# Filter spectra of a convolution block from high and low float32r parts instead of four-byte floats

## The chip, the core and the metric

The kernel runs on one core of a Trainium2 chip. A core has TensorE (PE; its weight loads are listed as PEld), VectorE (DVE), ScalarE (ACT), GpSimd (POOL) and SyncE (SP), each with a queue of its own that runs in order, and 16 DMA engines. The metric is the device time of one launch in microseconds (us). The profile shows one execution; its span is counted from the first to the last instruction.

## The reference

An image batch `x` of 16 x 128 channels x 16 x 16 runs through a convolution with filters that depend on the image, an attention and a mixture of experts. Only the first part is touched. Cut to what matters:

```
query   = x.reshape(b, c, hw)                      # x group-normalised
key     = softmax(einsum('bchw,oc->bohw', x, K_w) + K_b)
filters = einsum('bcn,bnk->bck', query, key)       # 7 x 7 taps per image and channel
filters = einsum('bcij,oc->boij', filters, conv0_w) + conv0_b
filters = relu(layernorm(filters) * ln_w + ln_b)
filters = einsum('bcij,oc->boij', filters, conv1_w) + conv1_b
out     = depthwise_conv(x, filters, padding=3)    # 7 x 7, per image and channel
t = x + out;  t = t + attention(ln(t));  t = t + moe(ln(t))   # top 2 of 8 experts
```

## The kernel before

The images are taken in 8 pairs. The depthwise convolution is done in the frequency domain on a 19 x 19 grid: TensorE multiplies the image (`features_spectrum`, L1095) and the filters (`filter_spectrum`, L1163) by constant matrices of cosines and sines, VectorE multiplies the two spectra (`products`, `spectrum`, `rest_products`), and `image` (L1178) transforms back. The 181 frequencies need four result tiles: real and imaginary parts of 121 frequencies (tiles 0 and 1) and two tiles with the other 60 (124 rows each). Tiles 0 and 1 of the filter lie in PSUM bank `bank_d0`, tiles 2 and 3 in `bank_d1`. The constant matrix for the filter is `tapf`, 49 taps by 121 + 121 + 124 + 124 = 490 columns; the filter `filt` has 49 taps by 2 images by 128 channels.

Every engine has its own program, written by hand; the order in it is the order in which it runs, and semaphores tie the engines together. A loop over nine rounds `i` is a pipeline: in round `i` pair `i` is at stage n (normalisation), `i-1` at a (keys and filter taps), `i-2` at b (filter), `i-3` at c (convolution), `i-4` at d (attention), `i-5` at e (routing) and `i-6` at f (dispatch). After the loop the rest of the pairs stands in a list written out for each engine, and then come 71 blocks of 128 tokens through the experts.

What surrounds the change:

- VectorE's `filter_of(b)` (L820) adds the bias to the filter from PSUM and writes `filt`, near the end of round `i`. Behind it on VectorE come `slot_indices_of` (L789), `z_of(c)` (L838), `attention_sum(d)` (L852), `attention_stats(d)` (L662 to L669) and `weight_differences` (L678, L679). The statistics let GpSimd compute `ln2_rstd` (L459; the profile calls it `ln_rstd`).
- In the next round VectorE's `rows_of(e)` (L723) waits for that, writes the normalised rows, and TensorE's `router_input(e)` (L1103) transposes these rows. Then follow `scores` (L1170), `router` (L1110), and on VectorE `logits_of` (L730).
- TensorE in a round: transposes of `gbuf` (L1204), keys (L1209), `first_conv` (L1145), `filter_spectrum` (L1163) of the filter made in the round before, transposes of `z` (L1140), `filter_mean` (L1149), `features_spectrum` (L1095), `router_input` (L1103), `scores` (L1170), `router` (L1110), `filter_square` (L1153), an expert's weights (L1188), `kprob` transposes (L1277), group mean (L1283), `image` (L1178), ranks (L1120, L1122), L1296, L1303, `attention` (L1132), and `filter_of` (L1158), which makes the filter that L820 reads.
- `keep_busy` (L1090) are products whose results nobody reads.
Of the kernel before, what the change touches and what calls it, by code (L numbers as in the profile page):

```python
# [29 lines left out]
F32R = mybir.dt.float32r  # L30
# [6 lines left out]
P = 128  # L37
# [3 lines left out]
KKP = 64  # L41
# [33 lines left out]
def constants():  # L75
# [27 lines left out]
    tapf[:KK] = np.concatenate([re[:, :WIDE], im[:, :WIDE], both(re, im), both(im, re)], 1)  # L103

# [22 lines left out]
def build(nc, a_in, out):  # L127
# [9 lines left out]
    with ctx:  # L137
# [12 lines left out]
        tapf = cst("tapf")  # L150

# [11 lines left out]
        c1_b = sb("c1_b", [KK, C])  # L163
# [48 lines left out]
        frelu = sb("frelu", [P, 2, KK])  # L212
        filt = sb("filt", [KK, 2, C])
# [75 lines left out]
        filt_psum, filt_done = sem("filt_psum"), sem("filt_done")  # L289
        ghat_psum, ghat_done = sem("ghat_psum"), sem("ghat_done")  # L290
# [64 lines left out]
        with nc.Block() as block:  # L355
# [148 lines left out]
            def _(act):  # L504
                act.dma_start(b1c[:, :], a_in["b1c"]).then_inc(ld_bias, 16)
                act.dma_start(bgv[:, :], a_in["bgv"]).then_inc(ld_bias, 16)
                act.dma_start(c1_b[:, :], a_in["c1_b"].partition_broadcast(KK)).then_inc(ld_c1b, 16)
# [21 lines left out]
                def first_conv(b):  # L529
# [6 lines left out]
                    last.then_inc(f0_done, 1)  # L536

# [30 lines left out]
                for i in range(rounds):  # L568
# [52 lines left out]
                    if n is not None:  # L621
# [7 lines left out]
                        last.then_inc(g_done, 1)  # L629
                first_conv(7)  # L630
# [6 lines left out]
                weights_exp(4)  # L637
                rest_spectrum(7)
# [16 lines left out]
            def _(dve):  # L655
                dve.memset(ones[:, :], 1.0)
                dve.memset(either[:, TILES, :], 0.0)

# [152 lines left out]
                def rectified(b):  # L811
                    dve.wait_ge(fln_done, b + 1)
                    dve.tensor_scalar(frelu[:, :, :], fln[:, :, :], 0.0, None, ALU.max).then_inc(frelu_done, 1)

                def filter_of(b):
                    if b == 0:
                        dve.wait_ge(ld_c1b, 16)
                    dve.wait_ge(filt_psum, b + 1)
                    after(dve, what_psum, 2 * b)
                    dve.tensor_tensor(filt[:, :, :], bank_b[0:KK, 256:512].rearrange("k (s c) -> k s c", s=2),  # L820
                                      spread(c1_b[:, :], 1, 2), ALU.add).then_inc(filt_done, 1)

# [50 lines left out]
                for i in range(rounds):  # L873
# [111 lines left out]
                    if c is not None:  # L985
                        z_of(c)
                    if d is not None:
# [42 lines left out]
                second_choice(4)  # L1030
# [52 lines left out]
            def _(pe):  # L1083
# [770 lines left out]
```

## Time and profile before

| | us |
|---|---|
| runs | 331.98, 333.33, 332.0 (median 332.0) |
| profiled execution, its own time | 332.57 |
| its span | 330.6 |
| TensorE busy / weight loads | 296.0 / 236.5 |
| VectorE busy | 232.8 |
| ScalarE busy | 144.5 |
| GpSimd busy | 164.7 |

Busy time is the sum over the whole span, and matmuls are pipelined, so that a busy TensorE says little about whether it sets the time. From 7 us on TensorE runs almost without a gap; the rounds 3 to 8 start on it at 36.3, 53.5, 72.3, 92.9, 113.5 and 134.0 us, the list after the loop at 154.4, and the first expert block at 200.9.

### The profile page before, as it was taken

What the parts mean: (1) busy time and instruction counts of PE and PEld (TensorE: products, weight loads), DVE (VectorE), ACT (ScalarE), POOL (GpSimd) and SP (SyncE); (2) the same over time, 40 slices, a digit from 0 to 9 for tenths busy, and PEclk for the clock granted to TensorE, in tenths of its full rate; (3) what the DMA queues carried; (4) which work ended last, traced back from release to release, by engine and by line L of the source; (5) the groups of instructions that cost most, each with busy time, mean ns of one, the idle gap of its engine ahead of it and who ended that gap; (6) DMA issues with size and microseconds to landing.
All of it is one profiled execution on the core that took longest, in us unless ns stands there. A gap on an engine that the chain in (4) does not pass through costs nothing.

```text
span 330.6 us, 7141 instructions
## 1 busy us (share of the span) xinstructions
PE 296.0 (90%) x1733; PEld 236.5 (72%) x1733; DVE 232.8 (70%) x1012; ACT 144.5 (44%) x465; POOL 164.7 (50%) x187
## 2 busy tenths in 40 slices
PE   0889999999999999999998986999999999999910
PEld 0557777688777778778876764876888888888810
DVE  2424375679788797877889795688666676767883
ACT  1344343625237352461420424555566666666600
POOL 3000002021163746636748765667777777676650
PEclk9979999999999999999999998799999999999985
DMA  6751423050211811001101113334433333335937
GB/s 189 281 171 45 133 76 102 4 168 5 80 48 34 285 39 35 16 24 36 34 25 50 44 41 93 99 98 108 113 92 104 89 105 108 97 84 153 353 131 250
DMA packets 29920, 33.39 MB, mean 101 GB/s; under 512 B 5064, under 2 KB 23836, under 8 KB 29626
## 3 DMA queue, kind: packets, MB, share of 16 engines
q1 hardware_dynamic: 24608, 23.64, 24.3%
q0 software_dynamic: 4352, 8.60, 7.6%
q10 hardware_dynamic: 922, 0.71, 0.7%
q8 instruction: 16, 0.26, 0.4%
q14 instruction: 22, 0.18, 0.2%
HBM read 21.69 MB, written 11.68 MB: 101 GB/s over the span
## 4 chain that ended last, share of the span: by engine, by line
PE 65%; DVE 16%; issue 6%; POOL 4%; DMA 3%; ACT 3%; DVEq 1%; POOLq 0%; SPq 0%; ACTq 0%
PE bank L1784 7%; PE bank L1178 6%; PE bank L1095 6%; PE bank L1188 4%; PE bank L1759 4%; PE bank L1764 4%; PE bank L1760 4%; PE bank L1773 4%; PE bank L1163 3%; PE bank L1170 3%; PE bank L1090 3%; POOL rows_dram L429 3%; PE bank L1754 2%; DVE ys L1699 2%; PE bank L1132 2%
## 5 line engine op out<-in xcount | busy, mean ns | idle before, releaser
L1492 POOL DMA_INDIRECT moe_dram<-ys,xs x71 | 70.0, 987 | 29.0 <-issue 19.5
L429 POOL DMA_INDIRECT rows_dram<-row,slot x56 | 55.6, 993 | 24.6 <-issue 13.5
L1784 PE MATMUL bank<-w_all,gatedt 128*128 x284 | 44.1, 278 | 0.1
L1580 ACT ACTIVATE silu<-bank 128x256 f32<-128x256 f32 x71 | 27.2, 383 | 33.3 <-PE bank L1764 32.9
L1699 DVE SCALAR_TENSOR_TENSOR ys<-b_all,xs,bank 128x128 f32<-128x128 f32 x71 | 24.7, 348 | 23.0 <-issue 20.5
L1716 DVE SCALAR_TENSOR_TENSOR gated<-bank,xs,silu 128x256 f32<-128x256 f32 x71 | 34.2, 482 | 7.4 <-ACT silu L1580 3.4
L1784 PEld LDWEIGHTS bank<-w_all,gatedt 128*128 128x128 f32 x284 | 37.7, 193 | 0.3 <-issue 0.3
L1759 PE MATMUL bank<-w_high,x_high 128*128 x71 | 34.8, 491 | 2.6 <-ACT x_high L1567 2.6
L440 POOL TENSOR_TENSOR frstd<-fvar,minus_half 128x2 f32<-128x2 f32 x7 | 4.9, 706 | 52.4 <-DVE fvar L802 52.4
L1764 PE MATMUL bank<-w_high,x_low 128*128 x71 | 29.5, 415 | 0.4
L1178 PE MATMUL bank<-zhat,const 121*128 121x256 f32 (+1 forms) x128 | 29.6, 383 | 0.1
L1760 PE MATMUL bank<-w_low,x_high 128*128 x71 | 28.4, 400 | 0.0
L1773 PE MATMUL bank<-const,gated 128*128 128x128 f32 x142 | 27.9, 278 | 0.6 <-DVE gated L1716 0.6
L1571 ACT ACTIVATE gatedt<-bank 128x256 f32<-128x256 f32 x71 | 26.9, 379 | 1.2 <-PE bank L1773 1.1
L1773 PEld LDWEIGHTS bank<-const,gated 128*128 128x128 f32 x142 | 19.6, 142 | 9.5 <-DVE gated L1716 2.2
L1178 PEld LDWEIGHTS bank<-zhat,const 121*128 121x128 f32 (+1 forms) x128 | 23.6, 189 | 3.7 <-issue 0.5
L1567 ACT ACTIVATE x_high<-bank 128x128 fp32r<-128x128 f32 x71 | 19.7, 277 | 10.5 <-PE bank L1754 3.6
L1090 PE MATMUL bank<-const 128*128 128x256 f32 x82 | 23.5, 416 | 0.0
L1095 PE MATMUL bank<-gt,const 128*121 128x256 f32 (+1 forms) x96 | 22.8, 385 | 0.0
L1690 DVE TENSOR_TENSOR x_low<-bank,x_high 128x128 fp32r<-128x128 f32 x71 | 20.3, 286 | 3.3 <-ACT x_high L1567 3.2
L446 POOL TENSOR_TENSOR gn_rstd<-gn_var,minus_half 128x2 f32<-128x2 f32 x8 | 5.7, 715 | 32.1 <-DVE gn_var L966 32.1
L1764 PEld LDWEIGHTS bank<-w_high,x_low 128*128 128x128 f32 x71 | 13.6, 191 | 8.5 <-DVE x_low L1690 2.9
(203 smaller groups left out, 623.2 us busy)
## 6 DMA issues: line engine op xcount, KB each, us to landing
xs<-rows_dram SPq DMA_DIRECT2D x71, 66.0 KB, 1.9
xc<-in_x SPq DMA_DIRECT2D x8, 256.0 KB, 3.1
wgv<-in_wg SPq DMA_DIRECT2D x8, 256.0 KB, 2.8
wgv<-in_wv SPq DMA_DIRECT2D x8, 256.0 KB, 3.1
xt<-in_xt SPq DMA_DIRECT2D x4, 512.0 KB, 4.9
xt<-moe_dram SPq DMA_DIRECT2D x8, 256.0 KB, 4.5
moe_dram<-ys,xs POOLq DMA_INDIRECT x71, 2.3
const<-in_const SPq DMA_DIRECT2D x1, 1123.0 KB, 9.6
```

Of the source, the lines that this page charges most:

```text
L429: pool.indirect_dma_start(rows_dram, bass.IndirectOffsetOnAxis(ap=slot[:, f % 2, 2 * t + k:2 * t + k + 1], axis=0), row[:, f % 2, t, k, :] ...
L1090: pe.matmul(bank, ident, const[:, 0:2 * P], start=True, stop=True)
L1095: last = pe.matmul(bank_s[r // 2][0:tile_rows[r], r % 2 * 2 * C:(r % 2 + 1) * 2 * C], fwd[:, h, tile_cols[r]], gt[:, b % 2, h, :], start=( ...
L1178: last = pe.matmul(bank_o[:, h * 2 * C:(h + 1) * 2 * C], inv[0:tile_rows[r], r, h * P:(h + 1) * P], zhat[0:tile_rows[r], r, :], start=(r = ...
L1492: pool.indirect_dma_start(moe_dram, bass.IndirectOffsetOnAxis(ap=xs[:, u, C + 1:C + 2].bitcast(U32), axis=0), ys[:, u, :], None, bounds_ch ...
L1699: dve.scalar_tensor_tensor(ys[:, u, :], b2_all[:, bass.ds(e * C, C)], xs[:, u, C:C + 1], bank_y[j % 2][:, 0:C], ALU.mult, ALU.add).then_in ...
L1716: dve.scalar_tensor_tensor(gated[:, j % 2, :], bank_h[j % 2][:, HID:2 * HID], xs[:, j % U, C:C + 1], silu[:, j % 2, :], ALU.mult, ALU.mult ...
L1759: pe.matmul(bank_h[j % 2][:, :], x_high[:, j % 2, :], w_high[:, bass.ds(e * (2 * HID), 2 * HID)], start=True, stop=False)
L1760: pe.matmul(bank_h[j % 2][:, :], x_high[:, j % 2, :], w_low[:, bass.ds(e * (2 * HID), 2 * HID)], start=False, stop=False)
L1764: pe.matmul(bank_h[j % 2][:, :], x_low[:, j % 2, :], w_high[:, bass.ds(e * (2 * HID), 2 * HID)], start=False, stop=True).then_inc(S["h_psu ...
L1773: last = pe.transpose(bank_g[:, h * P:(h + 1) * P], gated[:, j % 2, h * P:(h + 1) * P], ident)
L1784: last = pe.matmul(bank_y[j % 2][:, 0:C], gatedt[:, j % 2, h * P:(h + 1) * P], w2_all[:, bass.ds(e * (2 * C) + h * C, C)], start=(h == 0), ...
```

## The change

The filter is written twice, to partitions 0 to 48 and 64 to 112 (`frelu` holds each tap twice, so that L1158 gives 113 rows, 15 of them zero taps with the bias). ScalarE copies all of it to a float32r tile, `filt_parts`, the high part (`filter_high`). VectorE then replaces partitions 64 to 112 by the difference between filter and high part (`filter_low`). The constant matrix is split once, at the end of round 2, into `tap_high` (which holds the taps twice as well) and `tap_low`. Each product of the spectrum becomes two in float32r: `tap_high` over 113 partitions, which sums high and low part of the filter, and `tap_low` with the high part over 49. The product of both low parts is left out. On TensorE the transposes of `z` move ahead of the spectra. After the loop `second_choice(4)` is written out, with `filter_low(7)` between its steps.

The constants and tiles:

```diff
+    tapf[KKP:KKP + KK] = tapf[:KK]
...
+        tap_high = sb("tap_high", [P, WIDTHS["tapf"]], F32R)
+        tap_low = sb("tap_low", [P, WIDTHS["tapf"]], F32R)
-        c1_b = sb("c1_b", [KK, C])
+        c1_b = sb("c1_b", [KKP + KK, C])
...
-        frelu = sb("frelu", [P, 2, KK])
-        filt = sb("filt", [KK, 2, C])
+        frelu = sb("frelu", [P, 2, 2, KKP])
+        filt = sb("filt", [KKP + KK, 2, C])
+        filt_parts = sb("filt_parts", [KKP + KK, 2, C], F32R)
```

ScalarE, with the calls at the end of a round (behind `gbuf`) and, last, after the loop (behind `weights_exp(4)`):

```diff
+                def filter_high(c):
+                    act.wait_ge(filt_done, c + 1)
+                    after(act, filt_low_done, low_of(c - 1))
+                    after(act, what_psum, 2 * c)
+                    act.activation(filt_parts[:, :, :].rearrange("k s c -> k (s c)"),
+                                   filt[:, :, :].rearrange("k s c -> k (s c)"), ACT.Copy).then_inc(filt_high_done, 1)
...
+                    if i == 2:
+                        act.wait_ge(ld_c2, 16)
+                        act.activation(tap_high[:, :], tapf, ACT.Copy).then_inc(filt_high_done, 1)
+                    if b is not None:
+                        filter_high(b)
...
+                filter_high(7)
```

VectorE, with the calls in a round (between `z_of(c)` and `attention_sum(d)`) and, last, after the loop:

```diff
+                dve.memset(frelu[:, :, :, :], 0.0).then_inc(filt_low_done, 1)
...
-                    dve.tensor_scalar(frelu[:, :, :], fln[:, :, :], 0.0, None, ALU.max).then_inc(frelu_done, 1)
+                    dve.tensor_scalar(frelu[:, :, :, 0:KK], spread(fln[:, :, :], 2, 2), 0.0, None, ALU.max).then_inc(frelu_done, 1)
...
+                def filter_low(c):
+                    dve.wait_ge(filt_high_done, high_of(c))
+                    dve.tensor_tensor(filt_parts[KKP:KKP + KK, :, :], filt[KKP:KKP + KK, :, :], filt_parts[KKP:KKP + KK, :, :],
+                                      ALU.subtract).then_inc(filt_low_done, 1)
...
+                    if i == 2:
+                        dve.wait_ge(filt_high_done, 1)
+                        dve.tensor_tensor(tap_low[:, :], tapf, tap_high[:, :], ALU.subtract).then_inc(filt_low_done, 1)
+                    if b is not None:
+                        filter_low(b)
...
                 filter_of(7)
-                second_choice(4)
+                chosen_of(4)
+                either_of(4)
+                filter_low(7)
+                exp_sum_of(4)
+                exp_reciprocal_of(4)
+                weights_of(4)
```

TensorE; in the round `features_of_z(d)` with its waits now stands ahead of the last lines:

```diff
-                        last = pe.matmul(bank_b[0:KK, 256 + s * C:256 + (s + 1) * C], frelu[:, s, :], c1_t, start=True, stop=True)
+                        last = pe.matmul(bank_b[0:KKP + KK, 256 + s * C:256 + (s + 1) * C],
+                                         frelu[:, s, :, :].rearrange("p d k -> p (d k)")[:, 0:KKP + KK], c1_t, start=True, stop=True)
...
-                        last = pe.matmul(bank_d[half][0:tile_rows[r], r % 2 * 2 * C:(r % 2 + 1) * 2 * C],
-                                         tapf[0:KK, tile_cols[r]], filt[:, :, :].rearrange("k s c -> k (s c)"),
-                                         start=True, stop=True)
+                        into = bank_d[half][0:tile_rows[r], r % 2 * 2 * C:(r % 2 + 1) * 2 * C]
+                        pe.matmul(into, tap_high[0:KKP + KK, tile_cols[r]], filt_parts[:, :, :].rearrange("k s c -> k (s c)"),
+                                  start=True, stop=False)
+                        last = pe.matmul(into, tap_low[0:KK, tile_cols[r]], filt_parts[0:KK, :, :].rearrange("k s c -> k (s c)"),
+                                         start=False, stop=True)
...
-                        pe.wait_ge(filt_done, c + 1)
-                        if c == 0:
-                            pe.wait_ge(ld_c2, 16)
+                        pe.wait_ge(filt_low_done, low_of(c))
```

On TensorE, the start of a round from 5 on (the names are tiles; L1140 and L1184 are the transposes of `z`, L1163 and L1209/L1211 the spectra), before:

```order
L1145 MATMUL bank<-fraw,small 128x98 [waits fraw_done,pos_done,filt_done]
L1163 MATMUL bank<-filt,const 121x256 [waits zhat_done,wlow_done,prod_done,filt_done]
L1163 MATMUL bank<-filt,const 121x256
L1163 MATMUL bank<-filt,const 124x256 x2
L1140 MATMUL bank<-const,z 128x128 [waits qt_done,z_done,z2t_done,gt_done]
L1140 MATMUL bank<-const,z 128x128 x3
L1149 MATMUL bank<-fsum,const 128x2 [waits f0_done]
```

and now:

```order
L1189 MATMUL bank<-fraw,small 128x98 [waits fraw_done,pos_done,filt_done]
L1184 MATMUL bank<-const,z 128x128 [waits qt_done,z_done,z2t_done,gt_done]
L1184 MATMUL bank<-const,z 128x128 x3
L1209 MATMUL bank<-filt_parts,tap_high 121x256 [waits zhat_done,wlow_done,prod_done,filt_low_done]
L1211 MATMUL bank<-filt_parts,tap_low 121x256
L1209 MATMUL bank<-filt_parts,tap_high 121x256
L1211 MATMUL bank<-filt_parts,tap_low 121x256
L1209 MATMUL bank<-filt_parts,tap_high 124x256
L1211 MATMUL bank<-filt_parts,tap_low 124x256
L1209 MATMUL bank<-filt_parts,tap_high 124x256
L1211 MATMUL bank<-filt_parts,tap_low 124x256
L1193 MATMUL bank<-fsum,const 128x2 [waits f0_done]
```

Four products became eight, the transposes of `z` stand ahead of them, and the spectra wait for the low part in place of the filter itself.

On VectorE, the end of a round (`t` is the attention sum, `ln_raw` its statistics), before:

```order
L820 TENSOR_TENSOR filt<-bank,c_b 49x256 [waits what_psum,filt_psum]
L789 CAST slot<-slotf 128x8 [waits route_step]
L838 TENSOR_SCALAR z<-t,ln_mv,ln_rstd 128x128 [waits attn_psum,ln_rstd_done]
L838 TENSOR_SCALAR z<-t,ln_mv,ln_rstd 128x128 x3
L852 SCALAR_TENSOR_TENSOR t<-bank,arec,t 128x128 [waits attn_psum,arec_done]
```

and now:

```order
L849 TENSOR_TENSOR filt<-bank,c_b 113x256 [waits filt_low_done,filt_psum]
L815 CAST slot<-slotf 128x8 [waits route_step]
L872 TENSOR_SCALAR z<-t,ln_mv,ln_rstd 128x128 [waits attn_psum,ln_rstd_done]
L872 TENSOR_SCALAR z<-t,ln_mv,ln_rstd 128x128 x3
L854 TENSOR_TENSOR filt_parts<-filt,filt_parts 49x256 [waits filt_high_done]
L886 SCALAR_TENSOR_TENSOR t<-bank,arec,t 128x128 [waits attn_psum,arec_done]
```

One instruction stands between `z` and the attention sum, and it waits for ScalarE.

## Rows read from the trace of the kernel before

**Rows 1.** The page, section 4: shares of the chain that ended last.

```profile
PE 65%; DVE 16%; issue 6%; POOL 4%; DMA 3%; ACT 3%; DVEq 1%; POOLq 0%; SPq 0%; ACTq 0%
```

**Rows 2.** Stretches: busy us and count by engine, granted clock, DMA share, GB/s.

```profile
36.20:53.50 17.30, 17.24 (x87) 13.33 (x87) 9.88 (x40) 5.99 (x20) 2.40 (x3) 1.00 0.28 90
...
205.00:210.00 5.00, 4.74 (x20) 3.78 (x21) 2.98 (x13) 2.37 (x8) 3.78 (x5) 0.50 0.45 110
```

**Rows 3.** Chain of waits, round 7: start, length, piece.

```profile
115.10 1.92 PE bank L1163 x8
```

**Rows 4.** Timeline of TensorE, expert blocks: start, length, instruction, count.

```profile
240.29 0.39 PE L1760 MATMUL bank<-w_low,x_high 128*128 x1
240.52 0.39 PE L1764 MATMUL bank<-w_high,x_low 128*128 x1
...
240.97 0.61 PE L1784 MATMUL bank<-w_all,gatedt 128*128 x4
241.42 0.27 PE L1754 MATMUL bank<-const,xs 128*128 128x128 f32 x1
```

**Rows 5.** Timeline of all engines, round 7.

```profile
113.24 0.42 DVE L820 TENSOR_TENSOR filt<-bank,c_b 49x256 f32<-49x256 f32 x1 [0.82 <-PE bank L1158]
...
114.68 1.11 DVE L852 SCALAR_TENSOR_TENSOR t<-bank,arec,t 128x128 f32<-128x128 f32 x4
...
117.40 1.22 POOL L459 TENSOR_TENSOR ln_rstd<-ln_var,minus_half 128x4 f32<-128x4 f32 x1 [0.99 <-DVE ln_var L669]
...
118.65 1.27 DVE L723 TENSOR_SCALAR row<-t,ln_mv,ln_rstd 128x127 f32<-128x127 f32 x4 [0.30 <-POOL ln_rstd L459]
...
120.04 0.57 PEld L1103 LDWEIGHTS bank<-const,row 128*128 128x128 f32 x4
...
120.25 0.60 PE L1103 MATMUL bank<-const,row 128*128 128x128 f32 x4
...
120.67 0.41 DVE L701 TENSOR_TENSOR prod<-bank,ghat 121x256 f32<-121x256 f32 x1
...
120.89 1.99 PE L1170 MATMUL bank<-qt 128*128 128x256 f32 x8
...
121.00 0.41 DVE L702 TENSOR_TENSOR prod<-bank,ghat 121x256 f32<-121x256 f32 x1
...
122.83 0.74 DVE L870 BATCH_NORM_STATS2 gn_raw<-xc 128x6 f32<-128x256 f32 x2
...
123.71 0.19 DVE L730 COPY logits<-bank 128x32 f32<-128x32 f32 x1
```

**Rows 6.** Timeline of VectorE, rounds 5 and 8: reading the logits.

```profile
82.61 0.19 DVE L730 COPY logits<-bank 128x32 f32<-128x32 f32 x1 [0.28 <-PE bank L1110]
...
144.25 0.19 DVE L730 COPY logits<-bank 128x32 f32<-128x32 f32 x1 [0.80 <-PE bank L1110]
```

**Rows 7.** Groups by form: busy us, mean ns, idle time before.

```profile
L521 ACT ACTIVATE row<-row 128x512 f32<-128x512 f32 x8 | 5.0, 628 | 0.0
...
L813 DVE TENSOR_SCALAR frelu<-fln 128x98 f32<-128x98 f32 x8 | 1.7, 213 | 0.1
```

**Rows 8.** Timeline after the loop: VectorE, TensorE and GpSimd.

```profile
163.86 1.13 DVE L852 SCALAR_TENSOR_TENSOR t<-bank,arec,t 128x128 f32<-128x128 f32 x4 [0.58 <-PE bank L1132]
...
168.33 0.19 DVE L755 TENSOR_TENSOR either<-chosen 128x32 bf16<-128x32 f32 x1
...
169.56 1.12 PE L1163 MATMUL bank<-filt,const 49*121 49x256 f32 x4
...
170.62 0.19 PE L1120 MATMUL bank<-either,before 128*128 128x40 bf16 x1
...
170.94 0.16 DVE L773 TENSOR_TENSOR base<-base,bank 128x8 f32<-128x8 f32 x1 [0.88 <-PE bank L1122]
...
172.28 1.03 POOL L429 DMA_INDIRECT rows_dram<-row,slot  x1 [3.88 <-DVE slot L789]
...
205.26 0.79 PE L1759 MATMUL bank<-w_high,x_high 128*128 x1 [2.24 <-ACT x_high L1567]
```

More of the change, by code:

```diff
@@ L289, in build, with high_of, low_of @@
         filt_psum, filt_done = sem("filt_psum"), sem("filt_done")
+        filt_high_done, filt_low_done = sem("filt_high_done"), sem("filt_low_done")
+        def high_of(c):
+            return c + 2
+        def low_of(c):
+            return c + 3
         ghat_psum, ghat_done = sem("ghat_psum"), sem("ghat_done")
@@ L506, in _ @@
                 act.dma_start(bgv[:, :], a_in["bgv"]).then_inc(ld_bias, 16)
-                act.dma_start(c1_b[:, :], a_in["c1_b"].partition_broadcast(KK)).then_inc(ld_c1b, 16)
+                act.dma_start(c1_b[:, :], a_in["c1_b"].partition_broadcast(KKP + KK)).then_inc(ld_c1b, 16)
                 act.dma_start(router_b[:, :], a_in["router_b"].partition_broadcast(1)).then_inc(ld_router, 16)
@@ L818, in filter_of @@
                     dve.wait_ge(filt_psum, b + 1)
-                    after(dve, what_psum, 2 * b)
-                    dve.tensor_tensor(filt[:, :, :], bank_b[0:KK, 256:512].rearrange("k (s c) -> k s c", s=2),
+                    if b > 0:
+                        dve.wait_ge(filt_low_done, low_of(b - 1))
+                    dve.tensor_tensor(filt[:, :, :], bank_b[0:KKP + KK, 256:512].rearrange("k (s c) -> k s c", s=2),
                                       spread(c1_b[:, :], 1, 2), ALU.add).then_inc(filt_done, 1)
+                def filter_low(c):
+                    dve.wait_ge(filt_high_done, high_of(c))
+                    dve.tensor_tensor(filt_parts[KKP:KKP + KK, :, :], filt[KKP:KKP + KK, :, :], filt_parts[KKP:KKP + KK, :, :],
+                                      ALU.subtract).then_inc(filt_low_done, 1)
                 def image_sum(c):
@@ L1216, in _ @@
                         first_conv(b)
+                    if d is not None:
+                        after(pe, gt_done, through(i, A))
+                        after(pe, z2t_done, through(i - 1, E))
+                        after(pe, qt_done, d)
+                        features_of_z(d)
                     if c is not None:
-                        pe.wait_ge(filt_done, c + 1)
-                        if c == 0:
-                            pe.wait_ge(ld_c2, 16)
+                        pe.wait_ge(filt_low_done, low_of(c))
                         after(pe, prod_done, c)
@@ L1226, in _ @@
                         filter_spectrum(c, 1)
-                    if d is not None:
-                        after(pe, gt_done, through(i, A))
-                        after(pe, z2t_done, through(i - 1, E))
-                        after(pe, qt_done, d)
-                        features_of_z(d)
                     if b is not None:
@@ L1329, in _ @@
                 pe.wait_ge(wlow_done, EXPERTS)
+                pe.wait_ge(filt_low_done, low_of(6))
                 filter_spectrum(6, 0)
@@ L1347, in _ @@
                 features_spectrum(7, (2,))
-                pe.wait_ge(filt_done, 8)
+                pe.wait_ge(filt_low_done, low_of(7))
                 filter_spectrum(7, 0)
```

2 lines of the change are left out of this document (added).

## The prediction

> **What bounds the kernel now.** I read the chain of waits first: two thirds of it is TensorE [rows 1]. The stretches say where. The loop of nine rounds (here named by the program's `i`) fills TensorE: 17.24 us busy of 17.30 in round 3 [rows 2]. That busy time is no proof that each TensorE instruction counts, so I went on to the timeline of all engines in a full round (round 7; rounds 5, 6 and 8 repeat it), looking for waits that only just do not happen. From the round in which routing starts (5), there is a ring through VectorE: filter bias `filt` (L820, released by TensorE), `z`, attention sum L852, its statistics, the power on GpSimd L459, the rows L723, and then the transposes of these rows on TensorE, L1103. The rows end at 118.65 + 1.27 = 119.92, the weight load of L1103 starts at 120.04, its product at 120.25 [rows 5]. So the rows arrive 0.2 us before TensorE is free. Everything that TensorE does between the start of a round and L1103, the filter spectra L1163 among it, lies beside this ring, and may shrink by only 0.2 us before TensorE waits for the rows. In rounds 3 and 4 there is no routing and no L1103, and TensorE alone sets the time. After the loop a list in written order follows in which VectorE, GpSimd and TensorE hand on to each other; then 71 expert blocks, which the change leaves alone.
>
> **What each part costs.**
>
> *The spectra on TensorE.* Removed: per pair 4 products of four-byte floats, 8 hardware products, 1.92 us, so 0.24 each [rows 3] (eight such stretches, two of them split). Added: 8 products in float32r of 256 columns. The trace has float32r only with 512 columns: starts 0.23 apart (240.29, 240.52), which bounds it from above; the four four-byte products of 128 columns, each with its own weight load, start 0.45 / 4 = 0.113 apart [rows 4], which is the fastest pace of any pair of load and product in these rows. Half of the 512 columns gives 0.115, and that lies beside the lower row; I take 0.115, so 8 x 0.115 = 0.92 and 1.0 us less per pair. The upper end, 0.23, would be 1.84 and 0.08 less.
>
> *The high and low part.* ScalarE copies 113x256 (`filter_high`), VectorE subtracts 49x256 (`filter_low`). ScalarE's SBUF copy of 512 columns takes 628 ns [rows 7]; at 256 between 0.31 (half) and 0.63, I take 0.42. In round 7 `filt` ends at 113.66; the copy would end near 114.15, and VectorE comes to `filter_low` at 114.68, behind `z` [rows 5]. So the copy is hidden, with 0.5 us to spare; behind it on ScalarE queues only the copy of TensorE's transposes, which have to be made first anyway. `filter_low` is not hidden: it stands ahead of the attention sum, in the ring. Its like, L701 (two inputs, 256 columns), takes 0.41, but the next one, L702, starts 0.33 after it [rows 5]; I take 0.34. Queued behind it: attention sum, statistics, GpSimd's power, rows, L1103. Bounds: 0.33 and 0.41.
>
> *The doubled filter.* The weight load of L1158 grows from 49 to 113 columns; only the first of its loads is uncovered, and L1158 releases `filt`: between 0 and 0.11 (one load and product of rows 4), I take 0.05 per round. The bias on 113 partitions in place of 49 has the same columns: nothing. `frelu` doubles from 98 to 196 elements, 213 ns now [rows 7], so between 0 and 0.21 more, I take 0.1; in the loop VectorE idles afterwards for the image, which hides it.
> By the Trainium skill ("VectorE: DVE Perf Modes", "The perf-mode tier table (the rule you actually need)") a four-byte tensor_scalar within SBUF runs two elements a cycle; kept here, an estimate by that page is 0.05 for the 98 further elements, and 0.15 if reading the input twice loses the mode. No row decides it, and the sum changes by 0.05 either way.
>
> *Once.* `tap_high` and `tap_low` (490 columns) stand at the end of round 2, ahead of the first parts; the copy is like that of 512 columns, 0.63 [rows 7]. TensorE has its transposes, keys and first convolution to do meanwhile. I take a wait of 0.1 in round 3, between nothing and one such step, 0.6. The larger load of `c1_b` and the memset lie in the opening wait for data.
>
> *The move of the `z` transposes* ahead of the spectra costs nothing on TensorE: the same instructions, and VectorE had left `z` at 114.68 [rows 5], before the 115.10 at which the spectra, and now the transposes, follow on TensorE [rows 3].
>
> **The sum.** Rounds 3 and 4: -1.0 + 0.1 + 0.05 and -1.0 + 0.05, together -1.8. Rounds 5 to 8: the ring grows by 0.34 + 0.05 = 0.39 each, and gives back only what idles in it. Where do the rows go next? TensorE: L1103, then the scores L1170 at 120.89, where four products at 0.113 would have let it start at 120.70; with the 0.2 ahead of L1103, TensorE has room for 0.35. VectorE: from the rows' end it works without a pause to the image statistics, 122.83 + 0.74 = 123.57, and reads the logits (L730) at 123.71 [rows 5]: room for only 0.14. So VectorE becomes the later one in rounds 6 and 7. In round 5 its wait for the logits is 0.28, in round 8 (no image statistics) 0.80 [rows 6], there TensorE's 0.35 holds. Growth: 4 x 0.39 - (0.28 + 0.14 + 0.14 + 0.35) = +0.65. The loop as a whole: -1.15.
>
> After the loop: the attention sum L852 of pair 5 waits 0.58 for TensorE [rows 8]; VectorE itself comes later by 0.34 + 0.1 there, so it can move by -0.1, and the image of pair 6 with it. Then come the spectra of pair 7, L1163 at 169.56, four of them in 1.06 us up to the ranks at 170.62 [rows 8]; at 0.115 they take 0.5 less. `filter_low(7)` is ready before: it stands on VectorE behind `either`, which starts at 168.33 [rows 8]. The ranks release L773, which waits 0.88 for them, and that releases GpSimd's dispatch, which waits 3.88 for its slots [rows 8]; GpSimd then sets the pace to the next `z`. So -0.6 more. The spectra of pair 6 save nothing: the scores behind them wait for VectorE's centred filters, which come later by `filter_low`.
>
> Total -1.15 - 0.6 = -1.75 us. Against the profiled execution, 332.57 us (span 330.6 and 1.97 around it), that is 330.8. The median of the runs before is 332.0, 0.57 lower; from there **330.3 us**.
>
> **Rivals.**
> 1. *All of it is kept*: `filter_low` finds a pause and the rows come in time, so 1.0 goes in each of six rounds, and the list gives 0.6: 332.0 - 6.6 = 325.4. For it: TensorE's busy share. Against: 0.2 us ahead of L1103.
> 2. *The ring takes back more*: ScalarE's copy comes later than VectorE's `z`, or the waits on semaphores cost more, say 0.25 in each of rounds 5 to 8: 330.3 + 1.0 = 331.3. For it: a ring through three engines that has no slack. Against: 0.5 us of room for the copy.
> 3. *Slower: float32r of 256 columns keeps the pace of 512*, 0.23. Rounds 3 and 4 then give 0.16 less 0.2, nothing; rounds 5 to 8 cost 0.65, the list 0.15: +0.85, 332.9. The sum turns from gain to loss at about 0.19 per product. For it: no row shows 256. Against: 0.113 per load and product at half the columns with two passes.
> 4. *The clock.* In rounds 5 to 7 TensorE now idles some 1.2 us ahead of L1103. The granted clock is 1.00 in round 3 and 0.50, that is 1.2 GHz, from 205 to 210, behind the gap of 2.24 us that ends at 205.26 [rows 2, 8]; that stretch of 5 us did the work of 2.5. One such fall costs about 2.5: 332.8. Against it: the new gap is half as long.
> The Trainium skill ("TensorE: Matmul & The Clock Gate", "Part 1: The HAM clock gate (the "warmup" mystery)") says that "the default state is throttled, and activity releases the throttle", which speaks against a change that takes work from TensorE without shortening the round.
> 5. *It does not do what it says*: both products and all parts stand in the changed order, so no chance is given.
>
> **How the numbers follow.** Forecast 0.55 (own range 329.4 to 331.2), rival 1 0.06, rival 2 0.22, rival 3 0.09, rival 4 0.08. Half a per cent, 1.7 us, is about what a measurement of this kernel can tell from no change, so faster means below 330.3. The forecast lies on that edge: 0.32 of it faster, 0.23 same. Faster 0.32 + 0.06 + a little of rival 2 = 0.40. Rivals 3 and 4 lie within or just past +0.5%: half of 4 and a third of 3 and some unknown, slower 0.09. Same 0.51. The range leaves out rival 1 and the tail of 4: 328.7 to 332.8.
>
> **What would show it.** Right: 0.11 to 0.12 between the starts of the new products; a round 3 and 4 shorter by 0.9 each; rounds 6 and 7 not shorter, with TensorE idle about 1.2 us and released by the rows; no wait of VectorE for `filter_high` in the loop; the ranks of pair 4 about 1.8 us earlier. Wrong: rounds 6 and 7 shorter by 0.5 or more, starts 0.2 apart, a granted clock below 1.00 inside the loop, or the expert stage changed in length by more than a few tenths.

## The result

The changed kernel takes 343.6 us (median of four runs, 339.81 to 345.39) against 332.2 for the kernel before on the same chip, ratio 1.03 (95% interval 1.0255 to 1.0344). Ratios and intervals, here and below, leave out slow runs, those over 1.5% above the fastest of their kernel (here 345.39); medians and ranges do not. It is 11 us slower where 1.75 faster was forecast. The profiled execution after took 343.45 us (span 341.7; before 330.6).

The chain of waits after says again that TensorE sets the time, and more of it [rows 1]:

```profile
PE 68%; DVE 16%; DMA 5%; ACT 4%; issue 4%; DVEq 1%; POOL 1%; SPq 0%; POOLq 0%; ACTq 0%
```

So I cut both traces at the same places on TensorE: the start of each round, the first convolution of the list (L1145, now L1189) and the first `w_high` product of the expert blocks (L1759, now L1805). Columns as in [rows 2]; the number before the last two is the granted clock. After:

```profile
0.00:37.78 37.78, 25.91 (x115) 18.58 (x115) 12.98 (x61) 12.38 (x33) 5.59 (x24) 0.95 0.54 171
37.78:59.24 21.46, 20.68 (x86) 15.31 (x87) 11.49 (x44) 6.69 (x22) 2.40 (x3) 0.84 0.25 71
59.24:78.50 19.26, 18.53 (x100) 14.42 (x101) 11.61 (x47) 8.19 (x29) 2.40 (x3) 1.00 0.24 76
...
120.47:141.42 20.95, 20.20 (x117) 15.97 (x118) 17.78 (x95) 9.47 (x32) 11.72 (x12) 1.00 0.14 50
141.42:163.70 22.28, 21.44 (x113) 16.57 (x113) 16.68 (x86) 8.40 (x31) 11.02 (x11) 0.92 0.08 25
163.70:212.34 48.64, 45.40 (x253) 35.81 (x254) 41.89 (x227) 15.17 (x51) 31.67 (x32) 0.96 0.12 39
212.34:341.70 129.36, 112.11 (x715) 93.58 (x715) 90.71 (x284) 68.12 (x215) 84.50 (x87) 0.92 0.44 131
```

Before, the same stretches (round 3 starts at 36.26):

```profile
36.26:53.47 17.21, 17.21 (x87) 13.30 (x87) 9.85 (x40) 5.99 (x19) 2.40 (x3) 1.00 0.28 90
53.47:72.33 18.86, 18.25 (x102) 14.37 (x101) 10.91 (x46) 8.04 (x28) 2.40 (x3) 1.00 0.25 77
...
113.50:134.04 20.54, 19.93 (x117) 15.91 (x118) 17.19 (x93) 9.16 (x31) 11.72 (x12) 1.00 0.18 66
134.04:154.36 20.32, 19.48 (x114) 15.45 (x114) 16.14 (x85) 8.07 (x29) 11.01 (x11) 1.00 0.09 28
154.36:201.60 47.24, 43.53 (x253) 34.35 (x253) 40.73 (x224) 14.35 (x49) 31.64 (x32) 1.00 0.13 40
201.60:330.60 129.00, 111.09 (x715) 92.99 (x715) 90.42 (x284) 68.16 (x215) 84.55 (x87) 0.93 0.45 131
```

The difference of 11.1 us is made up of +1.5 in the opening, +4.25 in round 3, +0.4 in round 4, +1.2 in rounds 5 to 7 (0.4 each), +2.0 in round 8, +1.4 in the list, and +0.4 in the blocks. Two things stand out: a steady 0.4 per round at full clock, and stretches in which the clock is lower than before.

The steady part is in the spectra. TensorE in round 7 after (start, length, instruction), to be read beside [rows 3] and [rows 5]:

```profile
122.27 0.36 PE L1209 MATMUL bank<-filt_parts,tap_high 113*121 113x256 f32 x1
122.56 0.38 PE L1211 MATMUL bank<-filt_parts,tap_low 49*121 49x256 f32 x1
...
124.71 0.38 PE L1193 MATMUL bank<-fsum,const 128*128 128x2 f32 x2
...
127.62 0.60 PE L1147 MATMUL bank<-const,row 128*128 128x128 f32 x4
```

and its weight loads:

```profile
122.24 0.18 PEld L1209 LDWEIGHTS bank<-filt_parts,tap_high 113*121 113x121 f32 x1
122.56 0.18 PEld L1211 LDWEIGHTS bank<-filt_parts,tap_low 49*121 49x121 f32 x1
```

The products start 0.305 apart, not 0.115. Each weight load starts only where the product before gives way (at 122.56, 0.29 behind that product's start), so the load of 0.18 is laid in front of each product instead of beside the one before. Eight products take 2.44 in place of 1.92. L1147, the transposes of the rows, follows without a wait, and so it does in every round: the ring through VectorE never came to bound a round.

The other part begins in round 3. All engines after:

```profile
39.03 0.42 ACT L554 ACTIVATE filt_parts<-filt 113x256 fp32r<-113x256 f32 x1 [0.80 <-DVE tap_low L1023]
39.48 0.42 DVE L854 TENSOR_TENSOR filt_parts<-filt,filt_parts 49x256 fp32r<-49x256 f32 x1 [0.54 <-ACT filt_parts L554]
39.96 0.38 PE L1209 MATMUL bank<-filt_parts,tap_high 113*121 113x256 f32 x1 [0.54 <-DVE filt_parts L854]
...
41.34 0.57 PE L1209 MATMUL bank<-filt_parts,tap_high 113*124 113x256 f32 x1
```

The high part waits for the split of the taps, TensorE waits 0.54 for the low part, and from about the fourth product on everything takes longer. The clock there:

```profile
40.90:49.00 8.10, 8.10 (x23) 5.92 (x23) 3.02 (x10) 0.97 (x3) 0.00 (x0) 0.58 0.00 0
```

8.10 us at 0.58 do the work of 4.70, if the work goes with the clock; so, by this estimate, 3.4 of the 4.25 lost in round 3 are the clock.

### The profile page after: what moved, and what is told of

It reads as the page before. It is cut to its first block, busy times and chain, and to the rows that moved or that the text cites. A ratio compares the mean times of both kernels' runs of the same rounds, so it can differ in the third digit from the quotient of the medians.

```text
span 341.7 us, 7169 instructions
## 1 busy us (share of the span) xinstructions
PE 304.7 (89%) x1733; PEld 242.2 (71%) x1733; DVE 238.6 (70%) x1022; ACT 147.4 (43%) x474; POOL 164.7 (48%) x187
## 4 chain that ended last, share of the span: by engine, by line
PE 68%; DVE 16%; DMA 5%; ACT 4%; issue 4%; DVEq 1%; POOL 1%; SPq 0%; POOLq 0%; ACTq 0%
PE bank L1225 9%; PE bank L1830 7%; PE bank L1139 7%; PE bank L1235 4%; PE bank L1805 4%; PE bank L1810 4%; PE bank L1806 4%; PE bank L1819 4%; PE bank L1217 4%; PE bank L1211 3%; PE bank L1134 3%; PE bank L1209 2%; DMA small<-in_small 2%; PE bank L1800 2%; PE bank L1154 2%
## 5 line engine op out<-in xcount | busy, mean ns | idle before, releaser
L1805 PE MATMUL bank<-w_high,x_high 128*128 x71 | 35.4, 499 | 2.0 <-ACT x_high L1613 2.0
L1225 PE MATMUL bank<-zhat,const 121*128 121x256 f32 (+1 forms) x128 | 30.5, 392 | 0.0
L1225 PEld LDWEIGHTS bank<-zhat,const 121*128 121x128 f32 (+1 forms) x128 | 24.6, 197 | 3.6 <-DVE t L886 0.2
L1139 PE MATMUL bank<-gt,const 128*121 128x256 f32 (+1 forms) x96 | 26.4, 430 | 0.0
L1134 PE MATMUL bank<-const 128*128 128x256 f32 x82 | 24.3, 427 | 0.0
L1139 PEld LDWEIGHTS bank<-gt,const 128*121 128x121 f32 (+1 forms) x96 | 19.5, 210 | 3.6
```

Of the source, the lines that this page charges most:

```text
L1134: pe.matmul(bank, ident, const[:, 0:2 * P], start=True, stop=True)
L1139: last = pe.matmul(bank_s[r // 2][0:tile_rows[r], r % 2 * 2 * C:(r % 2 + 1) * 2 * C], fwd[:, h, tile_cols[r]], gt[:, b % 2, h, :], start=( ...
L1225: last = pe.matmul(bank_o[:, h * 2 * C:(h + 1) * 2 * C], inv[0:tile_rows[r], r, h * P:(h + 1) * P], zhat[0:tile_rows[r], r, :], start=(r = ...
L1805: pe.matmul(bank_h[j % 2][:, :], x_high[:, j % 2, :], w_high[:, bass.ds(e * (2 * HID), 2 * HID)], start=True, stop=False)
```

## The experiments

Theories A to D, as the expectation below numbers them, are ways in which the load could lose its place beside the product: narrow weights, unequal rows, float32r itself, or one pace per product.

**The pace by itself.** Behind the last block, which leaves everything ahead of it as it is:

```diff
+        def group(weights, moving, banks_, rows, n):
+            for _ in range(8):
+                pe.matmul(bank_h[0][:, 0:2 * P], ident, ident_mean, start=True, stop=True)
+            for k in range(16):
+                w, m = weights[k % 2], moving[k % 2]
+                pe.matmul(banks_[k // 2 % 2][0:rows, 0:n], w, m, start=(k % 2 == 0), stop=(k % 2 == 1))
...
+        group((tap_high[0:113, 0:121], tap_low[0:49, 0:121]), (parts, parts[0:49, :]), two, 121, 256)
+        group((tap_high[0:113, 0:121], tap_low[0:113, 0:121]), (parts, parts), two, 121, 256)
...
```

> The changed kernel with twelve groups of 16 products put behind its last block, each group behind 8 four-byte products of 128x128 by 256 columns that keep the clock; the rest is as it is. It measures the disputed pace, start to start, by itself: in the loop the float32r spectra stand 0.305 us apart, and the load of the next weights (0.18) begins only when the product before has ended. Groups in order: (1) as in the loop, 113 and 49 rows by turns, 121 weight columns, 256 columns; (2) 113 rows in both; (3) 49 rows in both; (4) 113 rows, 128 weight columns; (5) 128 rows, 128 weight columns, 256 columns; (6) the same, 512 columns; (7) the same, 128 columns; (8) 128 rows, 121 weight columns; (9) 128 rows, 64 weight columns; (10) four-byte, 49 rows, 121 weight columns, 256 columns; (11) four-byte, 113 rows; (12) four-byte, 128x128. Theory A (weights narrower than 128 columns are not loaded ahead): 0.30 in groups 1, 2, 3, 8, 9, and 0.11 to 0.13 in 4 and 5. Theory B (a change of the number of rows stops it): 0.30 in group 1 alone, 0.11 to 0.13 in 2 to 5 and 8. Theory C (a float32r load never runs beside the product before it, so that each product costs its load of 0.18 and its columns): 0.29 to 0.31 in groups 1 to 5 and 8, 0.23 to 0.25 in group 7, 0.38 to 0.41 in group 6. Theory D (the forecast's own upper rival, float32r keeps one pace per product whatever its columns): 0.23 in 2 to 7. All theories: four-byte groups 0.22 to 0.25.

TensorE behind the last block (L1857 are the 8 four-byte products between the groups, L1860 the groups; lines of a group of equal shape are one row of 16):

```profile
326.34 0.38 PE L1860 MATMUL bank<-filt_parts,tap_low 49*121 49x256 f32 x1
326.65 0.38 PE L1860 MATMUL bank<-filt_parts,tap_high 113*121 113x256 f32 x1
...
330.94 5.41 PE L1857 MATMUL bank<-const 128*128 128x256 f32 x16
...
336.43 0.28 PE L1860 MATMUL bank<-filt_parts,tap_high 113*121 113x256 f32 x1
336.55 0.28 PE L1860 MATMUL bank<-filt_parts,tap_low 113*121 113x256 f32 x1
...
338.10 3.62 PE L1857 MATMUL bank<-const 128*128 128x256 f32 x16
...
357.82 4.07 PE L1860 MATMUL bank<-w_high,x_high 128*128 128x512 f32 x16
...
391.86 7.07 PE L1860 MATMUL bank<-filt,const 113*121 113x256 f32 x32
```

113 and 49 rows by turns: 0.31 apart. 113 in both, or 49 in both: 0.12. Narrow weights at equal rows change nothing (121 and 64 columns: 2.25 and 2.24 for 16). Theory B alone stands; A, C and D fall. The row of 512 columns, 4.07 for 16 or 0.24 apart, shows that the forecast's halving was right for equal rows (128 columns are no faster than 256, though: 1.92 from the first start of 16 to the start behind them). The fillers, as I call the 8 four-byte products, tell something more: behind the group of unequal rows the same 8 four-byte products took 5.41 in place of 3.62, at a granted clock of 0.66, so partly at 1.2 GHz:

```profile
325.94:330.94 5.00, 5.00 (x18) 2.84 (x16) 2.76 (x5) 0.00 (x0) 0.30 (x1) 1.00 0.61 191
330.94:336.00 5.06, 5.06 (x17) 4.16 (x17) 2.90 (x6) 0.00 (x0) 0.00 (x0) 0.66 0.69 258
```

**Which rows.** The same with other pairs, `group((x_high[0:a, 0, 0:128], x_high[0:b, 1, 0:128]), (w_high[0:a, 0:256], w_high[0:b, 0:256]), ...)`, where `a` and `b` are the numbers of rows:

> As the run that measured the pace by itself, with other groups of 16 float32r products of 256 columns behind the last block, 128 weight columns, the numbers of rows by turns: (1) 113 and 49, (2) 113 and 65, (3) 113 and 97, (4) 128 and 113, (5) 64 and 49, (6) 49 and 33, (7) 49 and 32, (8) 49 and 17, and (9) four-byte products of 113 and 49 rows by turns, 121 weight columns. Theory B1 (any change of the number of rows has the price): 0.30 in all of 1 to 8. Theory B2 (the array works in tiles of 32, 64 or 128 rows, a product takes the smallest that holds its rows, and only a change of that has the price): 0.30 in 1, 7 and 8, 0.12 in 2 to 6. In group 9 the price of 0.185 for each of 16 changes adds 3 us to the 7.1 of equal rows if it holds for four-byte products too, and nothing if it belongs to float32r.

TensorE, the groups in order; a row gives the shape of a group's first product:

```profile
329.19 6.18 PE L1860 MATMUL bank<-w_high,x_high 113*128 113x256 f32 x16
...
340.70 2.28 PE L1860 MATMUL bank<-w_high,x_high 113*128 113x256 f32 x16
...
357.12 2.19 PE L1860 MATMUL bank<-w_high,x_high 64*128 64x256 f32 x16
359.23 3.72 PE L1857 MATMUL bank<-const 128*128 128x256 f32 x16
362.88 2.18 PE L1860 MATMUL bank<-w_high,x_high 49*128 49x256 f32 x16
...
368.64 5.03 PE L1860 MATMUL bank<-w_high,x_high 49*128 49x256 f32 x16
373.60 5.38 PE L1857 MATMUL bank<-const 128*128 128x256 f32 x16
...
389.07 9.92 PE L1860 MATMUL bank<-filt,const 113*121 113x256 f32 x32
```

113 with 65 or 97, 128 with 113, 64 with 49 and 49 with 33 are quick (2.18 to 2.28 for 16); 113 with 49 (6.18, partly at the lower clock), 49 with 32 and 49 with 17 are slow (5.03 each). So it is the price that theory B2 forecast: the bounds lie at 32 and 64 rows, and only a step across one has it. Four-byte products pay it as well, where it was tried (113 and 49 rows): 9.92 for 16 against 7.07 with equal rows, 0.18 per change. The Trainium skill ("TensorEngine Tiling (Array Packing)", "Key Properties") has a sentence that the forecast had not weighed: "Changing tiling mode (not just tile) drains the TensorE". The runs fit it, with 0.185 per change; that the number of rows of a plain product chooses such a mode is read into them, and no trace names the mode. Each of the three slow groups was followed by a longer filler (5.75, 5.38, 5.37), none of the five quick ones (3.62 to 3.72).

**Another order of the same products**, high, high, low, low by turns into the two banks:

```diff
+                    for rs in ((0, 2), (1, 3)):
+                        for low in (False, True):
+                            for r in rs:
...
```

> The changed kernel with its eight spectra in the loop in another order: high, high, low, low, high, high, low, low, by turns into the two banks, so that the number of rows changes four times in a pair in place of eight. Theory B, a price of 0.185 for each change of rows in either direction: 1.7 us for the eight, 0.12 behind a product with as many rows and 0.305 behind one with other rows. If only the fall from 113 to 49 rows has the price: 1.2 to 1.4. If it was two products into the same place of PSUM, one behind the other: 0.12 in all.

TensorE in round 7:

```profile
118.02 0.48 PE L1226 MATMUL bank<-filt_parts,tap_high 113*121 113x256 f32 x2
118.43 0.49 PE L1221 MATMUL bank<-filt_parts,tap_low 49*121 49x256 f32 x2
```

0.42 for each two, 1.68 for eight, in both directions alike; 336.4 us in one run. As theory B has it (one gap of 0.12 and one of 0.305 make 0.42), and it is not two products into one place of PSUM.

**Equal rows in the kernel**, alone and with the taps split earlier:

```diff
-                        last = pe.matmul(into, tap_low[0:KK, tile_cols[r]], filt_parts[0:KK, :, :]...
+                        last = pe.matmul(into, tap_low[0:KKP + KK, tile_cols[r]], filt_parts[:, :, :]...
```

The product of both low parts is then summed too, at no cost.

> The changed kernel with one edit: the product of the low taps takes 113 rows too (both parts of the filter) in place of 49, so that no product of the spectra differs from its neighbour in rows. Theory B (a change of the number of rows keeps the next weights from being loaded beside the product): spectra 0.12 apart in place of 0.305, so 1.5 less in each of 8 pairs; with fewer sparse stretches the clock also falls for less time. If TensorE stays the bound of each round: 12 less than 343.6, so 331 to 332, and less still by what the clock gives back, down to 329. If the ring through VectorE takes back 0.65 of each pair in rounds 5 to 8, as the forecast had it: rounds of 20.5 to 20.6 in place of 20.95 and 333 to 335. Rival: what holds in a group of 16 like products does not hold between other work, pace 0.25 to 0.30, total above 341.

333.4 us, ratio 1.0027 (1.000 to 1.0055): some 10 of the 11 us are gone with one edit. Rounds 5 to 7 are 20.70 to 20.77 long, so it is the second of the cases expected: TensorE no longer bounds them, the ring does. In round 3 the wait of 0.54 is still there, and the clock no longer falls:

```profile
38.98:55.82 16.84, 16.06 (x87) 12.83 (x87) 11.49 (x44) 6.68 (x22) 2.40 (x3) 1.00 0.29 88
```

The early taps alone (`tap_high` ahead of the copy of `fraw` in round 2, `tap_low` behind `gn_var`, in place of at the round's end):

> The changed kernel with the two parts of the taps made earlier in the third round (high on ScalarE ahead of the copy of the raw filter, low on VectorE behind the variance of the group norm) in place of at its end, so that the first filter's parts do not stand behind them. Theory 1 (the wait of 0.54 to 0.7 us in front of the first spectra, with the sparse products behind it, is what lets the clock fall to 0.62 from 40 to 49 us): no such wait, granted clock 1.00 in that round, the round 17.8 long in place of 21.4, total 343.6 less 3 to 4, so 339.5 to 341. Theory 2 (the float32r products are themselves what lets it fall, wherever they stand): the wait goes, the clock still falls there, total less 0.5 to 1, so 342.5 to 343.2.

338.6 us, ratio 1.018 (1.0123 to 1.0235), below the ranges of both theories. The wait is gone, the clock still falls in round 3, but for less time: both theories had a part.

```profile
36.65:55.92 19.27, 19.03 (x87) 14.41 (x87) 10.82 (x43) 6.29 (x21) 2.40 (x3) 0.91 0.25 76
```

Both together:

> The edit of the same rows and the taps made earlier in the third round, together. The early taps alone gave 338.6. If the two add up: 338.6 less 12, so 326 to 328, under the kernel before by 4 to 6; if the ring takes back 0.65 in four rounds: 329.5 to 331; if nothing but the spectra were late and the clock falls in the list as in the changed kernel: 331 to 333.

332.8 us, ratio 1.0006 (0.9983 to 1.003): no difference from before. The two edits don't add up to 326 to 328, since most of what each takes away is the same loss. Round 3 of the four profiles, one execution of each kernel, shows it: 21.46 long with unequal rows and the wait (clock 0.84), 19.27 with unequal rows alone (0.91), 16.84 with the wait alone (1.00) and 16.12 with neither (1.00). So the wait alone does not let the clock fall and the unequal products do; the wait in front of them makes the fall longer. The stretches with both edits:

```profile
0.00:37.68 37.68, 26.25 (x116) 18.92 (x116) 13.65 (x62) 12.88 (x34) 5.95 (x24) 0.95 0.56 173
37.68:53.80 16.12, 15.88 (x86) 12.81 (x87) 10.82 (x43) 6.29 (x21) 2.40 (x3) 1.00 0.29 91
53.80:71.54 17.74, 17.00 (x101) 13.93 (x101) 11.61 (x47) 8.18 (x29) 2.40 (x3) 1.00 0.26 82
...
113.00:133.76 20.76, 18.61 (x117) 15.38 (x118) 17.57 (x95) 9.80 (x32) 11.72 (x12) 1.00 0.17 64
```

Rounds 3 and 4 gain 1.09 and 1.12, and round 7 loses 0.22. There the loads lie beside the products again (the load for the product at 115.00 starts 0.08 behind the start of the one before), and the ring bounds, with TensorE idle:

```profile
114.80 0.36 PE L1209 MATMUL bank<-filt_parts,tap_high 113*121 113x256 f32 x1
114.88 0.19 PEld L1211 LDWEIGHTS bank<-filt_parts,tap_low 113*121 113x121 f32 x1
115.00 0.28 PE L1211 MATMUL bank<-filt_parts,tap_low 113*121 113x256 f32 x1
...
120.03 0.63 PE L1147 MATMUL bank<-const,row 128*128 128x128 f32 x4 [1.23 <-DVE row L749]
```

**The transposes of `z` put back behind the spectra**, in that kernel:

> As the kernel with same rows and early taps, and the transposes of z put back behind the spectra, where the kernel before has them. If their place ahead of the spectra was worth nothing: the same as that kernel within 0.7. If it is what keeps TensorE from waiting for the filter's parts in each round: a wait of 0.1 to 0.4 ahead of the first spectra of each round, total 1 to 2 longer. If it costs (z's transposes wait for z ahead of the spectra): 0.5 to 1.5 shorter.

332.8 us, ratio 0.9997 (0.9979 to 1.0016): the move is worth nothing.

**The wider load of the bias**, in the kernel before (113 in place of 49 partitions), and put later in the kernel with early taps:

> The kernel before with one edit: the bias of the filter loaded onto 113 partitions (56.5 KB) in place of 49 (24.5 KB); nothing reads the added rows. Theory 1 (the wider load delays the small constants, which land at 7.03 in place of 5.24 us and start TensorE 1.8 later): 333.5 to 334.2 against 332.2, first product at 8.6 to 8.9. Theory 2 (the landing of the first loads varies from run to run or hangs on something else): 332.0 to 332.5, first product at 7.0 to 7.2.

> As the kernel with the early taps, and the load of the filter's bias issued only when the first two loads of constants have landed. If the wider load is what delays the small constants: 1.5 to 1.9 less than the kernel with the early taps alone, first product at 7.0 to 7.2. If not: the same as that kernel within 0.5.

The first came out 334.4, ratio 1.0056 (1.0017 to 1.0095), with its first product at 8.72; the second 339.0, no better than 338.6. The first product came at 6.45 to 7.03 in three profiles with the narrow load, at 6.80 to 8.83 in those with the wide one, and at 7.54 and 8.22 with the wide one issued late. The load may cost up to 1 to 2 us at times; that it causes the +1.5 of the opening is not shown.

**Relieving the ring.** First the spectra behind `features_spectrum`, and `filter_low` behind `attention_stats`, in all rounds; then also `filter_of` ahead of `attention` on TensorE:

> The kernel with same rows and early taps, with the spectra of the filters behind the spectra of the features on TensorE, and the low part of the filter behind the statistics of the attention's output on VectorE (in place of ahead of its sum). Theory (the ring through VectorE bounds rounds 5 to 8: 20.76 a round with 18.61 of TensorE busy, and the low part's 0.46 lies on it): those rounds 20.3, total 2 less than 332.8, so 330.5 to 331.3. Rival (rounds are bound by something else on the way, a transfer of VectorE's work to a later place only shifts the wait): rounds 20.7 to 20.8, total as before, 332.5 to 333.

> As the kernel with the late spectra, and the product of the filter (4 products, 0.6) ahead of the attention's 16 (1.9) on TensorE, so that VectorE's bias of the filter no longer waits 0.69 for it. Theory of the ring: 0.2 to 0.35 less again per round (z then waits for the power on GpSimd), rounds 19.9 to 20.1, total 329 to 330.5, faster than the kernel before by 0.5 to 1 percent. Rival: the ring is then closed by TensorE and the group norm, rounds stay at 20.3.

332.2, ratio 1.0011 (0.9989 to 1.0033), and 333.2, ratio 1.0006 (0.9972 to 1.004): no gain in the total, although round 7 is 20.24 and 20.04 long in place of 20.76, as the theory of the ring had it. Round 3 became 17.37 long (16.12), and in the list TensorE, now waiting for the late low part, stood idle, and the clock fell behind that. In the second of them:

```profile
156.00:158.00 2.00, 0.00 (x0) 0.00 (x0) 1.87 (x11) 0.55 (x2) 0.75 (x2) 1.00 0.10 34
158.00:160.00 2.00, 1.92 (x8) 1.68 (x9) 1.33 (x4) 0.56 (x4) 1.80 (x2) 0.73 0.00 0
```

The same with the bias loaded late:

> As that, and the load of the filter's bias issued only behind the first constants. If the wider load is what cost 1.9 in the kernel before (0.6 to 3.2), 1 to 2 less; if the early part varies for other reasons, the same within 0.7.

It gave 332.4, ratio 0.999 (0.9947 to 1.0034). The median is 0.7 lower, which these intervals don't tell from nothing. The kernel before with `filter_of` ahead of `attention` alone:

> The kernel before with the product of the filter ahead of the attention on TensorE and nothing else: what the reordering gives without the change. Rounds 5 to 8 of before are 20.55 with 19.93 of TensorE busy, so there is 0.6 to gain at most in each: 330.5 to 332 if the ring bounds them too, 332 to 332.8 if TensorE does.

332.3, ratio 1.0005 (0.9984 to 1.0026): without the change this move gives nothing. The other move, the spectra behind those of the features, was not tried in the kernel before.

**The moves only where they pay**, and fillers for TensorE's gap in the opening:

```diff
-                    if b is not None:
+                    if b is not None and not 3 <= i < PAIRS:
                         filter_low(b)
...
                         if a == 0:
-                            keep_busy(bank_o[:, 0:2 * P], 1)
+                            keep_busy(bank_o[:, 0:2 * P], 4)
...
-                            keep_busy(bank_o[:, 0:2 * P], (0, 1, 5)[i])
+                            keep_busy(bank_o[:, 0:2 * P], (0, 2, 5)[i])
```

> Same rows, early taps, product of the filter ahead of the attention, and the late spectra and late low part only where they pay: spectra behind the features from round 4 on, low part behind the statistics in rounds 3 to 7, both early in the others (late in round 3 they cost 1.25, late in round 8 they left TensorE 2 us without work in the list, and the clock fell there). If what the equal pace saves (0.96 a pair) is lost in the ring of rounds 5 to 8 and nowhere else: round 3 16.1, rounds 5 to 7 20.05, list 47.5, total 332.8 less 2.5 to 3, so 329.5 to 330.5, faster than the kernel before by 0.5 to 0.9 percent. If each microsecond taken from TensorE is given back by the clock in the list: 332 to 333.

> As that, with three more filling products in the opening's wait for the softmax of the keys (0.95 to 1.9 of idle TensorE at 15 to 17 us, behind which the clock stood at 0.50 from 19.5 to 23 in most profiles) and one more in the wait for the group norm. If that gap is what lets the clock fall in the opening: no fall there, 1 to 1.5 less than without them, 328.5 to 329.5. If it falls anyway, or the fillers come too long: the same or 0.5 more.

> The kernel before with the same fillers alone, so that what they give is not put down to the change: if the opening's fall of the clock goes, 330.8 to 331.3 against 332.2; if not, 332 to 332.7.

330.3, ratio 0.9937 (0.9916 to 0.9958); with fillers **328.0, ratio 0.9866 (0.984 to 0.9892)**; the kernel before with the same fillers 332.3, ratio 0.9994 (0.9974 to 1.0015). The first two are faster than the kernel before by 0.6 and 1.3 per cent, with intervals that lie below 1. The second:

```profile
0.00:36.97 36.97, 26.56 (x123) 19.09 (x123) 13.65 (x62) 12.97 (x34) 5.94 (x24) 1.00 0.57 176
...
110.63:130.68 20.05, 18.79 (x117) 15.53 (x118) 17.55 (x94) 9.68 (x33) 11.67 (x13) 1.00 0.15 53
```

The ring gave back 0.7 a round. What the fillers do is less clear: in both profiles the opening's clock is 1.00. The run times (327.7 to 329.4 against 328.7 to 331.7) and the mean granted clock of the runs (0.966 to 0.971 against 0.956 to 0.965) say that the clock falls less with them; that it is the opening's fall is not shown. In the kernel before they shorten the profiled opening (round 3 starts at 34.50) and not the median.

## Why the prediction was wrong

*The pace of the spectra* is the step that failed. "0.23 apart ..., which bounds it from above" was taken from [rows 4], where every product has 128 rows; the rows of the new products, 113 and 49 by turns, were not looked at. The pace was 0.305, so the eight products took 2.44 in place of the 0.92 of the sum. With equal rows it is 0.12, the value that the forecast took (0.115). Rival 3 had the right sign by the wrong mechanism: its turning point of 0.19 was passed, but float32r of 256 columns does not keep the pace of 512. Its sum has a slip, too: four spectra at 0.23 take 0.92 in place of 1.06, so the list would gain 0.14 there and not cost 0.15.

*The rows of 128 around the spectra* pay too: L1193 behind them holds TensorE for 0.25 up to the next product (124.71 to 124.96), and for 0.14 in the kernel with equal rows.

*The clock.* Rival 4 named it, for gaps ahead of L1103 that never came. It fell behind the unequal products, in round 3, where they stand behind the wait, and again in round 8, where there is none. Round 3 alone lost an estimated 3.4 to it, against the forecast's 2.5 for one fall; more went in round 8 (0.92) and in the list (0.96). Behind the same eight products in rounds 4 to 7 it stayed at 1.00; what decides between those rounds and 3 and 8 is open. How much of round 8 and of the list is the clock was not separated further.

*Once.* The split of the taps made TensorE wait 0.54 where 0.1 was taken (the bound of 0.6 held); not counted was that `filter_high` queues behind `tap_low` (0.80 at 39.03).

*High and low part.* Right: the copy took 0.42 and was hidden. `filter_low` takes 0.42 and the next instruction starts 0.45 after it (121.64, 122.09), so 0.34 was too little and its upper bound of 0.41 too.

*frelu, the doubled filter, the move of `z`.* 0.27 in place of 0.213, so 0.06 more, near the lower of the two estimates (0.05 and 0.15), and hidden; no cost of L1202 seen apart; the move worth nothing. As forecast.

*The sum*, once the pace is 0.12: rounds 3 and 4 -2.2 (forecast -1.8); rounds 5 to 8 +0.1, +0.2, +0.2, -0.1, together +0.4 (forecast +0.65), with TensorE waiting 1.23 for the rows (forecast about 1.2). That mechanism was right. The list, forecast -0.6, gave +0.3 (47.54 against 47.24), and the opening was 1.4 longer. These two took what was left of the gain. Up to the ranks the list went as forecast: they start 15.74 behind its start (169.70, 153.96) in place of 16.26 (170.62, 154.36), and GpSimd's dispatch stays 0.6 ahead of before. The lead is lost at VectorE's last rows, which start at 197.13 (before at 197.22) and, by the profile, wait there for a DMA that scatters earlier rows:

```profile
197.13 1.11 DVE L749 TENSOR_SCALAR row<-t,ln_mv,ln_rstd 128x127 f32<-128x127 f32 x4 [0.45 <-DMA rows_dram<-row,slot]
```

The forecast followed the list only as far as GpSimd's next `z`.

*What no run tested.* The kernel before pays for changes of rows too: its products of 49 rows stand between products of 128. Its eight hardware products take 1.92 [rows 3], where eight behind others of 49 rows take 1.77 (32 from 381.21 to 388.30 in the first experiment). From the first convolution to the features' spectra it takes 2.94 in round 7 (L1145 at 114.64, L1095 at 117.58), and the kernel with equal rows and early taps 1.83 (114.14, 115.97). Of these 1.11, two changes at 0.18 would be 0.36, an estimate. The filter of the kernel before, padded to 113 rows and left in four-byte floats, would have told what float32r itself gives.

## What to carry over

Before two kinds of product are interleaved on TensorE, compare their numbers of rows: if they lie on two sides of 32 or 64, pad the smaller one, since rows of zeros or of a term that is wanted anyway are free and the change is not. A pace read from rows bounds another only where the shapes agree in every dimension, not just in the one that was changed. And where a ring through other engines has no slack, faster products first become idle TensorE; it took the reordering of the ring to turn them into time (332.8 us, ratio 1.0006, became 330.3, ratio 0.9937).

## What the runs showed of the hardware

- Products of more than 64 rows, of 33 to 64, and of 32 or fewer are three classes here. A float32r product behind one of another class starts 0.185 later (0.305 against 0.12 for 256 columns): its weight load is not laid beside the product before. Four-byte products of 113 and 49 rows pay 0.18. Not tried: 32 rows or fewer beside more than 64, and two products of 32 or fewer.
- Busy time does not show it: TensorE counts as busy for 5.00 of 5.00 us in the slow group too. The distance of starts, and of weight loads, does.
- Behind a group of 16 float32r products at that pace the granted clock fell each time, to 0.62 to 0.68 over the longer fillers (4 of 4), and behind the groups of equal class never (15 of 15), although both count as busy. Of the rounds of the changed kernel, each with eight such products, it fell in 3 and 8 and stayed at 1.00 in 4 to 7.
